# Spreading the gated second half of a three-stage image pipeline between the channel pairs of the first convolution

## What is computed

```
x_proj = einsum('bchw,oc->bohw', x, proj_w)                     # 128 -> 64 channels
att1 = route(x_proj, [3x3, 5x5] depthwise)                      # one kernel picked per sample
att2 = route(att1,   [7x7, 9x9, 11x11] depthwise, dilation 3)   # one kernel picked per sample
out  = concat([att1, att2], channel)                            # 128 channels
att  = conv7x7([mean over channels, max over channels]) -> sigmoid
gate = att[:, 0:1] + att[:, 1:2]
return out * gate + x
```

## Time and profile before

| | us |
|---|---|
| median of three runs | 6338.1 (6338.06 to 6348.23) |
| the profiled execution | 6353.46 |
| its span on the core | 6351.9 |
| busy: TensorE / VectorE / ScalarE / GpSimd | 4896.8 / 3135.5 / 2832.8 / 1256.7 |
| moved by DMA | 1285.33 MB, mean 202 GB/s |
| mean granted TensorE clock | 0.849 of full speed |

### The profile page before, as it was taken

How to read it: one execution, slowest core, us unless ns; L and a number is a source line. 1 busy time by engine, 2 the same in 40 slices (tenths; PEclk the granted TensorE clock), 3 DMA queues, 4 the chain that set the end, 5 groups by cost and what they waited for, 6 DMA issues and landing times.

```text
span 6351.9 us, 164601 instructions
## 1 busy us (share of the span) xinstructions
PE 4896.8 (77%) x62816; PEld 3336.1 (53%) x62816; DVE 3135.5 (49%) x3835; ACT 2832.8 (45%) x5378; POOL 1256.7 (20%) x2010
## 2 busy tenths in 40 slices
PE   5678897887878788787878888787887878885453
PEld 2236464655646465564745556464555646464342
DVE  3215445464545545464554545546544554645344
ACT  3455464544545455444544545354454535452120
POOL 2001011212112121211212121121212212121332
PEclk9889898898989889798988889898798979887675
DMA  9656758869697785968779696886969688696857
GB/s 225 182 133 188 174 160 217 228 182 237 191 229 198 215 223 179 227 212 217 210 194 231 180 230 207 214 227 172 233 181 242 199 217 234 179 224 156 226 131 189
DMA packets 1015814, 1285.33 MB, mean 202 GB/s; under 512 B 670750, under 2 KB 865737, under 8 KB 984414
## 3 DMA queue, kind: packets, MB, share of 16 engines
q1 hardware_dynamic: 855500, 578.24, 39.1%
q0 software_dynamic: 90800, 555.20, 28.2%
q10 hardware_dynamic: 69026, 146.11, 8.3%
HBM read 950.16 MB, written 456.70 MB: 221 GB/s over the span
## 4 chain that ended last, share of the span: by engine, by line
PE 36%; DMA 33%; DVE 11%; issue 10%; ACT 3%; POOL 2%; SPq 2%; ACTq 1%; POOLq 0%; DVEq 0%
DMA out_dram<-RX 15%; PE psC L984 13%; DMA RX<-in_x_dram 8%; DVE MM L1198 7%; DMA RX<-w_d 5%; PE psA L922 5%; PE psA L923 5%; PE psA L858 5%; PE psB L953 3%; PE psB L867 2%; DMA RX<-nat_d 2%; PE psB L932 2%; PE psB L963 2%; DVE RX L1274 1%; DVE L L1255 1%
## 5 line engine op out<-in xcount | busy, mean ns | idle before, releaser
L984 PE MATMUL psC<-RX 61*60 61x96 f32 (+7 forms) x49152 | 1457.6, 266 | 231.6 <-POOL RX L591 96.2
L984 PEld LDWEIGHTS psC<-RX 61*60 61x60 f32 x49152 | 1391.2, 132 | 304.3 <-issue 300.1
L1198 DVE TENSOR_REDUCE MM<-L 124x135 f32<-124x6480 f32 (+3 forms) x128 | 527.6, 4194 | 587.4 <-ACT L L775 587.4
L775 ACT ACTIVATE L<-psC 124x120 f32 (+4 forms) x2048 | 393.8, 284 | 830.0 <-PE psC L984 791.2
L858 PE MATMUL psA<-RX,projt 128*64 128x512 f32 x1920 | 577.0, 686 | 236.2 <-DMA RX<-in_x_dram 162.2
L922 PE MATMUL psA<-X,RX 128*128 128x240 f32 x1280 | 642.1, 591 | 125.4 <-ACT RX L740 125.3
L953 PE MATMUL psB<-ident,L 124*128 124x124 f32 x2160 | 445.5, 356 | 347.5 <-DVE RX L1274 286.6
L591 POOL COPY RX<-RX 64x720 f32<-64x720 f32 x512 | 402.3, 792 | 1455.4 <-DMA RX<-w_d 1454.4
L745 ACT ACTIVATE X<-psA,bias 128x246 f32<-128x246 f32 x1024 | 638.4, 737 | 62.6 <-PE psA L923 46.2
L923 PE MATMUL psA<-X,RX 128*128 128x240 f32 x1280 | 632.5, 583 | 0.0
L734 ACT ACTIVATE RX<-RX 32x640 f32<-32x640 f32 x320 | 233.8, 735 | 880.7 <-PE psA L923 749.9
(11 more groups left out here) (117 smaller groups left out, 5150.9 us busy)
## 6 DMA issues: line engine op xcount, KB each, us to landing
RX<-in_x_dram POOLq DMA_DIRECT2D x64, 2560.0 KB, 11.4
RX<-w_d ACTq DMA_DIRECT2D x512, 180.0 KB, 4.4
RX<-in_x_dram SPq DMA_DIRECT2D x128, 720.0 KB, 10.6
out_dram<-RX SPq DMA_DIRECT2D x128, 720.0 KB, 14.4
nat_d<-X SPq DMA_DIRECT2D x320, 280.0 KB
RX<-nat_d POOLq DMA_DIRECT2D x208, 400.0 KB, 6.8
RX<-in_x_dram POOLq DMA_DIRECT2D x416, 200.0 KB, 5.8
out_dram<-RX POOLq DMA_DIRECT2D x416, 200.0 KB, 4.9
```

The costliest lines, as they stand in the source:

```text
L775: ins = nc.scalar.activation(dst[:, 0:NU2 - par, 15 * r:15 * r + nq, par, :], src[:, par:BR:2, :, :], ACT.Identity)
L984: ins = nc.tensor.matmul(o[:, :, 0:kk, a:b], w2t[2 * q + p][rows, ch, z:z + PB], src[rows, 2 * p + ch, 0:nf, 3 * cg + dc:3 * cg + dc + kk, ...
L1198: nc.vector.tensor_reduce(dst[0:124, mm, :].rearrange("p (f b k) -> p f b k", f=9, k=3)[:, :, par:BR:2, :], src[:, :, 0:NU2 - par, :, par, ...
```

## The change

The table is now indexed by the channel pair (32 places) rather than by the group of four channels (16 places). The 16 f1 units keep their places, except that the first stands one pair earlier and the last four now stand behind pairs 25, 27, 29 and 30, where they stood behind 25, 25, 27, 29 (units 12, 13, 14, 15). f2 is no longer issued in five units of nine steps, behind pairs 5, 7, 9, 11 and 13, but in 23 chunks of two steps (the last of one), behind pairs 4 to 22; behind pairs 7, 11, 15 and 19 stand two chunks. Where f1 and f2 stand behind the same pair, f1 now comes first; before, f2 did. The wait for a unit's gated piece, VectorE's wait for the unit's x and the `gate2` of unit u+2 are at the same steps as before, now inside the chunks. In turn 17 the chunks alternate with f1 units, about two chunks to one unit. SyncE's, GpSimd's and ScalarE's programs are unchanged.

```diff
--- before.py
+++ after.py
@@ -59,15 +59,21 @@
 
 
 
-AFTER = {0: (("f1", 0),), 1: (("gt", 0), ("f1", 1)), 2: (("f2", 0), ("f1", 2)), 3: (("f2", 1), ("f1", 3)),
-         4: (("f2", 2), ("f1", 4)), 5: (("f2", 3), ("f1", 5)), 6: (("f2", 4), ("f1", 6)),
-         7: (("f1", 7),), 8: (("f1", 8),), 9: (("f1", 9),), 10: (("f1", 10),),
-         11: (("f1", 11),), 12: (("f1", 12), ("f1", 13)), 13: (("f1", 14),), 14: (("f1", 15),), 15: ()}
-
-AFTER_LAST = {0: (("gt", 0), ("f1", 0), ("f2", 0)), 1: (("f1", 1), ("f1", 2), ("f2", 1)), 2: (("f1", 3), ("f1", 4), ("f2", 2)),
-              3: (("f1", 5), ("f1", 6), ("f2", 3)), 4: (("f1", 7), ("f1", 8), ("f2", 4))}
-AFTER_LAST.update({g: (("f1", g + 4),) for g in range(5, 12)})
-AFTER_LAST.update({g: () for g in range(12, 16)})
+STEPS2 = 9 * NU2
+AFTER = {pair: [] for pair in range(C2 // 2)}
+for _u, _pair in enumerate((0, 3, 5, 7, 9, 11, 13, 15, 17, 19, 21, 23, 25, 27, 29, 30)):
+    AFTER[_pair].append(("f1", _u))
+AFTER[3].insert(0, ("gt", 0))
+for _c in range((STEPS2 + 1) // 2):
+    AFTER[4 + _c - (_c + 1) // 5].append(("f2", _c))
+
+AFTER_LAST = {pair: [] for pair in range(C2 // 2)}
+AFTER_LAST[0] = [("gt", 0), ("f1", 0)]
+for _c in range((STEPS2 + 1) // 2):
+    AFTER_LAST[1 + _c].append(("f2", _c))
+for _u in range(1, NU1):
+    AFTER_LAST[2 * _u].append(("f1", _u))
+
 
 
 def conv_block(nc, x, proj_w, w1, b1, w2, b2, att1_w, att1_b, att2_w, att2_b, sp_w, sp_b, out):
@@ -940,11 +946,12 @@
                     ins = nc.tensor.transpose(psB[0][0:124, NT * f:NT * f + NT], Gp[:, f, 0:124], ident[0:NT, 0:NT])
                 ins.then_inc(g2_mm, 1)
 
-            def finish2(m, u):
-                wait_alone(pe, att2_gated, NU2 * m + u + 1)
-                for t9 in range(9):
-                    t = 9 * u + t9
+            def finish2(m, c):
+                for t in range(2 * c, min(2 * c + 2, STEPS2)):
+                    u, t9 = divmod(t, 9)
                     p, k = divmod(t9, 3)
+                    if t9 == 0:
+                        wait_alone(pe, att2_gated, NU2 * m + u + 1)
                     if t >= 2:
                         wait_alone(pe, f2_add, 45 * m + t - 1)
                     for f in range(3):
@@ -1002,15 +1009,14 @@
                         for hf in range(2):
                             spatial(m, hf)
                 pieces, halves = 0, 0
-                for g in range(NG):
+                for pair in range(C2 // 2):
                     if t.new:
-                        for pair in (2 * g, 2 * g + 1):
-                            conv1(s, pair)
-                    for what, u in t.after[g]:
+                        conv1(s, pair)
+                    for what, u in t.after[pair]:
                         if what == "f1" and t.one:
 
                             if t.two:
-                                wait_alone(pe, f2_add, 45 * m + 9 * halves)
+                                wait_alone(pe, f2_add, 45 * m + min(2 * halves, STEPS2))
                                 if halves == 0 and pieces > 0:
                                     wait_alone(pe, g2_ready, m + 1)
                                 if pieces == 0:
@@ -1255,13 +1261,14 @@
                 nc.vector.tensor_tensor(t, t, G2s[0:124, n * u:n * u + n].unsqueeze(2).broadcast_to([124, n, C2]),
                                         ALU.mult).then_inc(att2_gated, 1)
 
-            def finish2(m, u):
-                q = u % 2
-                rows = slice(0, 128 if u < 4 else 64)
-                dve.wait_ge(xf_loaded[q], xf_count(m, u))
-                for t9 in range(9):
-                    t = 9 * u + t9
+            def finish2(m, c):
+                for t in range(2 * c, min(2 * c + 2, STEPS2)):
+                    u, t9 = divmod(t, 9)
+                    q = u % 2
+                    rows = slice(0, 128 if u < 4 else 64)
                     p, k = divmod(t9, 3)
+                    if t9 == 0:
+                        dve.wait_ge(xf_loaded[q], xf_count(m, u))
                     dve.wait_ge(f2_mm, 45 * m + t + 1)
                     pv = psB[t % 2][rows, 0:372].rearrange("p (f z) -> p f z", f=3)
 
@@ -1279,6 +1286,8 @@
                         add(1, 1, 0, 3, 3)
                         ins = add(1, 1, 3, 1, 1)
                     ins.then_inc(f2_add, 1)
+                    if t9 == 8 and u < NU2 - 2:
+                        gate2(m, u + 2)
 
             def gate1(n, u):
                 q = u % 2
@@ -1335,8 +1344,6 @@
                                 gate2(m, 1)
                             else:
                                 finish2(m, u)
-                                if u < NU2 - 2:
-                                    gate2(m, u + 2)
                 if t.new:
                     reduce1(s)
                 if t.next:
```

## The result

The kernel after takes 6307.2 us (6302.2 to 6311.6, four runs) against 6343.2 for the kernel before, now also the median of four (6338.1 to 6348.2): 0.9943 of the time before, 95% interval 0.9926 to 0.9960, 36 us less. The forecast was 6251, 87 us less. Direction and range held; the size did not.

The account below looks back on a forecast made before the run. No single engine was taken as the bound (TensorE 36%, DMA 33%). About -6 us a full turn, -78 over 13, and -9 in turn 2 gave -87: 6251 us, own range 6190 to 6310, wider range 6165 to 6400.

Parts of the forecast that it names:

- bursts: f2's 45 steps in chunks of two, additions hidden by pairs: about 32 us become 20.4, saving 11.5 a full turn.
- handovers, f2 behind f1: f2 right behind f1 waits for f1's additions on psB, 1.27 us a place, 11.4 us a full turn.
- f1's own waits: f1's old waits behind f2 (5.5 us) go, and units 12 and 13, now placed apart, save 3 us.
- first chunk: f2's first steps, now behind pair 4, wait 4.0 us for VectorE instead of 1.1: cost 3 us a turn.
- load of x: x's store-then-load trip must fit one unit's pitch: waits 12.5 us against some 15 before, saving 2 a turn.
- last unit behind pair 30: f1's last unit, one pair later, makes ScalarE's weight loads and pair 30's output about 1.7 us later.
- the landings behind f2's end: SyncE's last landings, issued after about 3022, are done near 3050, before the last f1: hidden.
- the walk through turn 8: Following f2's units in time gave waits for x of 3.5, 9 and 0 us at units 2, 3 and 4.
- The slower rival: In full turns x's round trip sets the pitch of f2's units: +7 us a turn, about 6430; chance 0.26.
- The sign that I had given: In the profile after, VectorE would idle 3 to 9 us for x at steps 18, 27 and 36.
- f2's end: In the first convolution, f2 ends 135 to 140 us from the first pair; beyond 150 us refutes the forecast.
- turns 2 and 17: Turn 2: 143 us against 152, -9; turns 16 and 17, without pairs between: 0, bounds -8 and +25.

Follow-up runs that it names:

- e4: Kernel after, but f2 again in five units of nine steps ahead of f1, turn 17 in its old order; 6283.6 us, 0.9925 of the kernel before.
- e8: Kernel after, but f1's stores write 200 of the 800 columns of each piece; 6237.0 us, 0.9845 of the kernel before.
- e1: Kernel after, but SyncE loads x ahead of the landings; 6254.6 us, 0.9872 of the kernel before.
- e13: Kernel after, but each landing cut to a quarter of its columns; 6152.0 us, 0.9701 of the kernel before.
- e5: Kernel after, but turns 3 to 16 have f2 in units of nine as in e4; turns 2 and 17 stay spread; 6253.1 us, 0.9870.
- e18: Kernel after with the later gate2 mid previous unit, gate1 behind the next pair's items, x loaded ahead of the landings; 6178.8 us, 0.9779.
- e14: e4 with each landing cut to a quarter of its columns; 6037.8 us, 0.9525 of the kernel before.

## Why the prediction was right or wrong

Terms of a full turn, forecast against the mean of the traces (idle time of TensorE, and time of its transposes from the start of one instruction to that of the next, less the idle time):

| term | forecast | measured |
|---|---|---|
| bursts | -11.5 | -8.5 (31.1 to 22.6) |
| handovers, f2 behind f1 | +11.4 | +10.5 |
| f1's own waits (old handovers, units 12 and 13) | -8.5 | -10.8 |
| first chunk | +3 | +3.2 (wait 4.2) |
| load of x, that is the long waits but the first chunk's | -2 | +4.2 (13.9 to 18.1) |
| f1's transposes, shorter | none | -1.1 |
| last unit behind pair 30 | +1.7 | +1.3 |

The first six add up to -2.5 us, which is what the first convolution changed by.

**Right.** The handovers: 1.00 to 1.42 us each, 10.5 together, from one row of another stage. The first chunk, from VectorE's order before. The last unit, and the landings behind f2's end. The DMA share, 0.95. f1's own waits fell by 10.8 us where I priced 8.5 (by 5.4 with the places alone, e4), and e4 shows that the places alone carry the gain of a full turn.

**Wrong, the load of x.** The step that failed is the walk through turn 8, which took each unit's start as the later of TensorE's arrival and the landing of x, and left VectorE's own order out. "The pair behind hides them" was said of gate2, and gate1 was counted only in the handovers. Of my 12.5 us for x 0.4 came; 17.7 us of something else did: VectorE's wait for nat_d, gate1, gate2 and its additions. The trips of 28.8, 34.9 and 30.0 us that I carried over were 29.8, 29.1 and 22.0 to the landing. The slower rival named the mechanism in a half sentence, f2's additions behind gate1 and its wait for nat_d, and priced the trip instead; its trips of 35 us did not come. The sign that I had given, VectorE's idle for x of 3 to 9 us at steps 18, 27 and 36, failed in turn 8, with none. Had I put gate1's rows into the walk, I would have seen 6.8 waits for nat_d a turn, 39 us, on VectorE in the kernel before: off f2's path there, since f2's additions did not stand behind them, and in TensorE's waits for f1 with only 4.0 us.

By the Trainium skill (DMA: Bandwidth & Descriptors, Queues, rings and completion order) f1's traffic on another queue takes turns with x's and would lengthen its trip; the trace bears that out in part at most. Issue to landing was 19.6 us for unit 2 (19.3 before), 18.9 for unit 3 (14.8) and 12.7 for unit 4 (11.0), while e8, with a quarter of f1's store bytes and all of its loads, had 17.4, 19.5 and 13.1. What moved it plainly is the traffic ahead of it in its own queue: for unit 2, 10.4 us with the landings behind it (e1) and 13.6 with a quarter of them (e13).

**Near misses.** f2's end, named at 135 to 140 us, came at 143.4 (104.1 before), short of the 150 that would have refuted me. The terms of the walk's first leg add up to 17.6 us, not 18.8, which changes no wait in it.

**Too high, the bursts.** The mechanism held and the term was 3.0 us too large. The chunks were taken at 0.81 us; the 23 of them average 1.05 by their length, since many run at a lower granted clock (last section).

**Wrong, turns 2 and 17.** Turn 2 gave 15.4 instead of 9. Its f2 steps (19.9 us after, with their short waits) and long waits (8.8) came as forecast (20.4 and about 8); what was wrong is the 115 us of turn 1 that they were added to. 7.7 of those are TensorE's waits for ScalarE's weights (L746), and in turn 2 after, with f2's steps between the pairs, 1.8 are left. Turn 17 gave 9.6 where I took 0, with -8 as the bound, though e4, with the old order there, shows that 4.2 of it came without the spreading; filling its gaps gave about 5. In e5, which spreads only these two, the end is 221.8 us (e4 230.3). That both erred to the good side, 16 us together, is luck, and it is why the time came within the range although a full turn gave a fifth of its forecast.

**Not settled.** Why the earlier load of x (e1) shortens the waits for nat_d too; that landings then start later is argued, not shown. Nor what bounds e18: its x waits, or its DMA share of 0.97. Nor what a later gate1 would give in the order of nine at once.

## What to carry to other kernels

When a burst is spread between other work, walk every engine's queue in program order, not only the resource that the burst waited for: a wait of a neighbour (here gate1's, 39 us a turn, all but 4 of them harmless) becomes the price once short dependent steps stand behind it. The releaser in a profile row is the instruction that came last; look one row further, at what held that one. And make the two halves of a change separately before crediting either: here the one that looked like tidying up carried the gain of a full turn, and the headline one cost 3 us. Moving gate1 brought the spread order from 178.9 to 173.0.

## What the runs showed of the hardware

The DMA view of turn 8 of the kernel after, 2894 to 3004 us: queues with packets, MB and share, then issues with count, KB and median us to landing.

```profile
q1 hardware_dynamic: 8605, 13.98, 55.1%
q0 software_dynamic: 2486, 10.58, 34.2%
...
L<-strip_d SPq DMA_DIRECT2D x8, 405.0 KB, 12.2
```

SyncE's queue (q1) takes 55.1% for 13.98 MB in 8605 packets, 3.9 points per MB, GpSimd's 34.2% for 10.58 MB in 2486, 3.2. The landings are the dear part: leaving out three quarters of them takes a turn of the nine-at-once order from 175.9 to 159.6 us (e14) and one of the spread order from 178.9 to 168.8 (e13), while three quarters of f1's store bytes were worth 4.1 there (e8).

The same six transposes took 0.81 us right behind a pair and 1.47 after 4 to 5 us of idle TensorE, a factor of 1.8. Windows over single instructions show why (the third number from the end of a row is the granted clock): two chunks of turn 8 after and the idle time ahead of the second, then the first f2 unit before.

```profile
2905.78:2906.59 0.81, 0.81 (x8) 0.81 (x7) 0.27 (x1) 0.00 (x0) 0.00 (x0) 1.00 0.87 329
2935.72:2940.87 5.15, 0.00 (x0) 0.03 (x1) 2.07 (x3) 0.18 (x1) 1.69 (x3) 0.50 0.99 265
2940.88:2942.35 1.47, 1.47 (x7) 1.47 (x8) 1.47 (x4) 0.00 (x0) 0.00 (x0) 0.50 1.05 303
```
```profile
2909.74:2916.91 7.17, 6.75 (x27) 4.58 (x27) 5.18 (x13) 2.11 (x4) 2.75 (x5) 0.50 0.70 177
```

The short chunk ran at a granted clock of 1.00 (2.4 GHz), the long one at 0.50 (1.2 GHz), and so did the idle time ahead of it. Over the 13 full turns after, 35 of the 36 chunks behind more than 1.5 us of idle time took 1.47 us. Behind a wait of 0.9 to 1.5 us, as at the handovers, 72 of 119 still took under 0.9 us, at 1.00, and 17 over 1.4, at 0.50 to 0.53. The first burst before (7.17 us for nine steps) ran at 0.50 as a whole, so the price of 7.7 us that the forecast read from it was that of the lower level.
